# A gated recurrence and a channel-mix FFN on eight cores: the a stage and the first LN1 moved ahead, LN1's staging on VectorE alone, wo's evictions on ScalarE

## The chip, the cores and the metric

The kernel runs on the eight NeuronCores of one Trainium2 chip. Each core takes one of the eight sequences of the batch; nothing is exchanged between them. The metric is the device time in microseconds of the slowest core. The cores form two dies, 0 to 3 and 4 to 7.

## The reference, cut to what matters

```python
# x: (8, 2048, 1024) fp32; eight sequences, one per core
h = layernorm(x)
h = rsqrt(sum(h*h) + eps) * h * gamma * sqrt(1024)
q, k, v, g = h @ wq, h @ wk, h @ wv, h @ wg
a = sigmoid(h @ wa)
y[t] = a[t] * y[t-1] + k[t] * v[t]          # scan over the sequence
x = x + (q * y * silu(g)) @ wo

h = layernorm(x); hp = h shifted by one token
xr = mu_r * h + (1 - mu_r) * hp
xk = mu_k * h + (1 - mu_k) * hp
r = sigmoid(xr @ W_r.T)
x = x + r * (square(relu(xk @ W_k.T)) @ W_v.T)
```

## The kernel before, in words

A core works through its 2048 tokens in eight blocks b = 0 to 7 of 256 tokens. All nine weight matrices stay on the chip in bf16. A matrix product ("stage", `mm_stage`, line 190) is 64 matmuls of 128x128 by 128x256 into four of the eight PSUM banks (`pp`); the stages take banks 0 to 3 and 4 to 7 in turn, so a stage can start only when the stage before the last has been evicted. Stages are named by their weights: k, v, q, a, g, wo, and for the FFN r (`wrT`), fk (`wkT`), fv (`wvT`). The results of wo and fv are brought back to token order by 16 TensorE transposes (line 205) and added to x (`resid_stage`, line 220).

A layer norm has two parts. `ln_stats` makes the statistics on VectorE, with one square root on ScalarE (line 256). `ln_apply` writes the normalized tile in bf16: the first 128 tokens by VectorE (line 287), the other 128 by ScalarE (line 292). It goes to `stg1` for the first norm (LN1, in `phase_A`) and to `bfP` for the second (in `phase_E1`, called E1 below). Two DMA transposes on the queue of SP (line 302), the second of which waits for the first, bring it into feature order: `xhat_fm`, one half for even and one for odd blocks, or `xh2_fm`. The program calls `phase_A(b + 2)` twice in an iteration b, once behind yq and once at its end; both do all the work and write the same values. The a stage of block b + 2 reads the first result, its k, v, q and g stages the second.

Blocks overlap. Iteration b runs wo, transposes and E1 of block b; k, v, q of b + 1; the token shift of b (`phase_E2xr`, `phase_E2xk`); kv, scan and yq of b + 1; r and fk of b; g of b + 1; fv, transposes and residual of b; the a stage of b + 2; the store of b and the load of x for b + 3. Each engine goes through its instructions in program order. The order is written out by hand; there is no scheduler. A small planner (`Plan`) notes for every named region its last writer and its readers, and puts a wait in front of an instruction for each of them:

```python
        for w in writes:
            reg = self.regions.get(w)
            if reg:
                if reg["w"]:
                    deps.add(reg["w"])
                deps.update(reg["r"])
```

Each matmul is a token of its own, so a region that a stage has read has 64 readers. When the waits are made, a token is left out only if its engine has already waited for a higher count of the same semaphore; they are gone through in rising order and by the names of the semaphores (dq.., scalar, tensor, vector):

```python
            for (sem, val) in sorted(rec["deps"]):
                ...
                if k.get(sem, 0) < cnt:
                    k[sem] = cnt
                    w.append((sem, wv))
```

and `run_engine` issues one wait instruction (`wait_ge`, line 572) for each.

Of the kernel before, what the change touches and what calls it, by code (L numbers as in the profile page):

```python
# [10 lines left out]
D = 1024  # L11
T = 2048
L = 256
NB = T // L
# [83 lines left out]
def build_program():  # L98
    nc = bass.Bass("TRN2", target_bir_lowering=False,
                   dynamic_dma_scratch_size=4096)  # L100
# [30 lines left out]
    xh2_fm = sb("xh2_fm", [128, NCH * L], BF16)  # L131
    bfP = sb("bfP", [128, NCH * L], BF16)
    stg1 = sb("stg1", [128, NTI * D], BF16)
    y2b = sb("y2b", [128, NCH * L], BF16)
    fA = sb("fA", [128, NCH * L], F32)
    fB = sb("fB", [128, NCH * L], F32)
    fC = sb("fC", [128, NCH * L], F32)
    stats = sb("stats", [128, 36], F32)
    gam = sb("gam", [128, NCH], F32)
    mur = sb("mur", [128, NCH], F32)  # L140
    muk = sb("muk", [128, NCH], F32)
# [8 lines left out]
    p = Plan()  # L150
# [13 lines left out]
    def chunked(t):  # L164
        return t[:, :].rearrange("p (c l) -> p c l", c=NCH)
# [104 lines left out]
    def ln_apply(b, which, tag):  # L270
        par = b % 3
        ssc = SS1 if which == 1 else SS2
        xreg = "x%d" % par
        reg = "stats%d" % which
        dstreg = ("xhf%d" % (b % 2)) if which == 1 else "xh2"
        bbc = BB1 if which == 1 else BB2
        stg = stg1 if which == 1 else bfP
        streg = "stg1" if which == 1 else "bfP"
        for ti in range(NTI):
            b_ap = stats[:, bbc + ti:bbc + ti + 1]  # L280
            m_ap = stats[:, (MV1 if which == 1 else MV2) + 2 * ti:
                         (MV1 if which == 1 else MV2) + 2 * ti + 1]
            s_ap = stats[:, ssc + ti:ssc + ti + 1]
            xt = x_tm[:, par, ti * D:(ti + 1) * D]
            if ti == 0:
                p.op("vector", (lambda xt=xt, m_ap=m_ap, s_ap=s_ap, stg=stg:
                                nc.vector.tensor_scalar(stg[:, 0:D], xt, m_ap, s_ap,
                                                        OP.subtract, OP.mult)),
                     reads=[xreg + "t0", reg], writes=[streg], tag=tag)
            else:  # L290
                p.op("scalar", (lambda xt=xt, b_ap=b_ap, s_ap=s_ap, stg=stg:
                                nc.scalar.activation(stg[:, D:2 * D], xt,
                                                     AF.Identity, bias=b_ap, scale=s_ap)),
                     reads=[xreg + "t1", reg], writes=[streg], tag=tag)
        for ti in range(NTI):
            if which == 1:
                dst = xhat_fm[:, b % 2, :].rearrange(
                    "p (c l) -> p c l", c=NCH)[:, :, ti * 128:(ti + 1) * 128]
            else:
                dst = chunked(xh2_fm)[:, :, ti * 128:(ti + 1) * 128]  # L300
            p.op("sync", (lambda dst=dst, ti=ti, stg=stg:
                          nc.sync.dma_start_transpose(
                              dst, stg[:, ti * D:(ti + 1) * D])),
                 reads=[streg], writes=[dstreg], dma=True, tag=tag + "_dmaT")
# [43 lines left out]
    def phase_A(b):  # L348
        ln_stats(b, 1, "A%d" % b)
        ln_apply(b, 1, "A%d" % b)  # L350

    def phase_hoist_a(b):
        rr = ["xhf%d" % (b % 2)]
        rhs = lambda kc, b=b: xhat_view(b, kc)
        a_ids = mm_stage("wa", rhs, rr, "a%d" % b)
        for j in range(4):
            p.op("scalar", (lambda j=j, a_ids=a_ids: nc.scalar.activation(
                fhalf(fA, j), pp[a_ids[j]][:, :], AF.Sigmoid)),
                 reads=["pp%d" % a_ids[j]], writes=["fA%d" % j], tag="siga%d" % b)
# [48 lines left out]
    def phase_ygy2(b, g_ids):  # L408
        for j in range(4):
            p.op("vector", (lambda j=j, g_ids=g_ids: nc.vector.tensor_tensor(  # L410
                fhalf(fC, j), fhalf(fC, j), pp[g_ids[j]][:, :], OP.mult)),
                 reads=["pp%d" % g_ids[j], "fC"], writes=["fC"], tag="yg%d" % b)
        p.op("vector", (lambda: nc.vector.tensor_tensor(
            y2b[:, :], fC[:, :], bfP[:, :], OP.mult)),
             reads=["fC", "bfP"], writes=["y2b"], tag="y2_%d" % b)

    def phase_D(b):
        wo_ids = mm_stage("wo", (lambda kc: chunked(y2b)[:, kc, :]), ["y2b"],
                          "wo%d" % b)
        for j in range(4):  # L420
            p.op("vector", (lambda j=j, wo_ids=wo_ids: nc.vector.tensor_copy(
                fhalf(fB, j), pp[wo_ids[j]][:, :])),
                 reads=["pp%d" % wo_ids[j]], writes=["fB%d" % j], tag="woev%d" % b)
        t_ids = transpose_stage(fB, "fB", "Tattn%d" % b, sub=True)
        resid_stage(b, t_ids, "resid1_%d" % b)

    def phase_E1(b):
        ln_stats(b, 2, "E1_%d" % b)
        ln_apply(b, 2, "E1_%d" % b)

    def phase_E2xr(b):
        v = chunked(xh2_fm)
        pv = chunked(bfP)
        xr = chunked(y2b)
        p.op("vector", (lambda v=v, pv=pv: nc.vector.tensor_copy(
            pv[:, :, 1:L], v[:, :, 0:L - 1])),
             reads=["xh2"], writes=["bfP"], tag="prev%d" % b)
        if b == 0:
            p.op("vector", (lambda pv=pv: nc.vector.memset(pv[:, :, 0:1], 0.0)),
                 reads=[], writes=["bfP"], tag="prev0_%d" % b)  # L440
        else:
            p.op("vector", (lambda pv=pv: nc.vector.tensor_copy(
                pv[:, :, 0:1], carry2[:, :].rearrange("p (c o) -> p c o", o=1))),
                 reads=["carry2"], writes=["bfP"], tag="prev0_%d" % b)
        p.op("vector", (lambda v=v: nc.vector.tensor_copy(
            carry2[:, :].rearrange("p (c o) -> p c o", o=1), v[:, :, L - 1:L])),
             reads=["xh2"], writes=["carry2"], tag="carry2_%d" % b)
        tsh = chunked(stg1)
        p.op("vector", (lambda: nc.vector.tensor_sub(
            stg1[:, :], xh2_fm[:, :], bfP[:, :])),  # L450
             reads=["xh2", "bfP"], writes=["stg1"], tag="xr%d" % b)
        for c in range(NCH):
            p.op("vector", (lambda c=c, tsh=tsh, pv=pv, xr=xr:
                            nc.vector.scalar_tensor_tensor(  # L454
                                xr[:, c, :], tsh[:, c, :], mur[:, c:c + 1],
                                pv[:, c, :], OP.mult, OP.add)),
                 reads=["stg1", "mur", "bfP"], writes=["y2b"], tag="xr%d" % b)
    def phase_E2xk(b):
        v = chunked(xh2_fm)
        pv = chunked(bfP)  # L460
        tsh = chunked(stg1)
        for c in range(NCH):
            p.op("vector", (lambda c=c, tsh=tsh, pv=pv, v=v:
                            nc.vector.scalar_tensor_tensor(  # L464
                                v[:, c, :], tsh[:, c, :], muk[:, c:c + 1],
                                pv[:, c, :], OP.mult, OP.add)),
                 reads=["stg1", "muk", "bfP"], writes=["xh2"], tag="xk%d" % b)

    def phase_F1(b):
        xr_fn = lambda kc: chunked(y2b)[:, kc, :]  # L470
# [17 lines left out]
    def phase_F3(b):  # L488
        ks_fn = lambda kc: chunked(xh2_fm)[:, kc, :]
        v_ids = mm_stage("wvT", ks_fn, ["xh2"], "fv%d" % b)  # L490
        for j in range(4):
            p.op("vector", (lambda j=j, v_ids=v_ids: nc.vector.tensor_tensor(
                fhalf(fB, j), pp[v_ids[j]][:, :], fhalf(fB, j), OP.mult)),
                 reads=["pp%d" % v_ids[j], "fB%d" % j], writes=["fB%d" % j],
                 tag="fvev%d" % b)
# [28 lines left out]
    for b in range(NB):  # L524
        phase_D(b)
        phase_E1(b)
        if b + 1 < NB:
            vq[b + 1] = phase_hoist_kvq_mm(b + 1)
        phase_E2xr(b)
        if b + 1 < NB:  # L530
            phase_kvev(b + 1, vq[b + 1][0])
        phase_E2xk(b)
        if b + 1 < NB:
            phase_scan(b + 1)
            phase_yq(b + 1, vq[b + 1][1])
        if b + 2 < NB:
            phase_A(b + 2)
        phase_F1(b)
        phase_F2(b)
        if b + 1 < NB:  # L540
            g_ids_of[b + 1] = phase_hoist_g(b + 1)
            phase_ygy2(b + 1, g_ids_of[b + 1])
        phase_F3(b)
        phase_F4(b)
        if b + 2 < NB:
            phase_hoist_a(b + 2)
        phase_G(b)
        if b + 2 < NB:
            phase_A(b + 2)
# [88 lines left out]
```

How the kernel before makes its waits and increments, by code:

```python
        def run_engine(eng_name, eng):  # L569
            for rec in per_engine[eng_name]:
                for (sem, val) in rec["waits"]:
                    eng.wait_ge(sems[sem], val)
                ins = rec["emit"]()
                if rec["inc"]:
                    step = 16 if rec["sem"].startswith("dq") else 1
                    ins.then_inc(sems[rec["sem"]], step)
# [17 lines left out]
        @block.sync  # L594
        def _(eng):
            run_engine("sync", eng)
            for (sem, val) in final_waits:
                eng.wait_ge(sems[sem], val)
```

## Time and profile before

| | |
|---|---|
| median of three runs | 840.29 us (838.47 to 850.4) |
| profiled execution, its own time | 843.49 us |
| its span, core 2 (slowest) | 842.0 us |
| spans of the eight cores | 830.3 to 842.0 us |
| TensorE busy on core 2 | 590.1 us (70%) |
| VectorE busy | 410.1 us (49%) |
| ScalarE busy | 161.2 us (19%) |
| mean granted TensorE clock, core 2 | 0.903 |

The profiled execution is one run of the program; its time is that of the whole launch, the span goes from the first to the last instruction of the slowest core. Busy TensorE time counts pipelined matmuls, so a stage is best read by the distance from its first matmul to the next stage's. The first 134 us are the loading of the weights and the first norm; then come the eight iterations.

### The profile page before, as it was taken

To read this page: it belongs to the slowest core of one execution; us is meant where nothing else is said; L and a number is where in the kernel's file an instruction comes from. 1 tells how busy PE (TensorE), PEld (TensorE's weight loads), DVE (VectorE), ACT (ScalarE), POOL (GpSimd) and SP (SyncE) were. 2 spreads that over 40 slices of the span, in tenths; PEclk is the share of its full clock that TensorE was granted. 3 is DMA by queue.
4 is the path that set the end of the run, shared out by engine and by line. 5 is a ranking of instruction groups with operands and counts; after the bars stand their busy time and mean duration, and the time that the engine had idled before them with its cause. 6 is when DMAs were issued, how large, how long until landed. Compare 5 with 4: busy or idle time off the path is not lost.

```text
span 842.0 us, 13591 instructions; the slowest of 8 cores (830.3 to 842.0 us)
## 1 busy us (share of the span) xinstructions
PE 590.1 (70%) x4864; PEld 505.1 (60%) x4864; DVE 410.1 (49%) x726; ACT 161.2 (19%) x230; POOL 5.1 (1%) x13
## 2 busy tenths in 40 slices
PE   0000005899968899969796979796969797989065
PEld 0000004778757678868686868685858686879054
DVE  0001730334656358465756565556565656546342
ACT  0000011122032210521142123212321232131121
POOL 2000000000000000000000000000000000000000
PEclk9999999988877778999989999899999988999679
DMA  9999994001003210141014101320032002201101
GB/s 170 175 186 168 165 170 68 1 2 8 19 2 76 75 26 1 27 126 26 7 21 126 26 14 41 98 26 14 25 114 26 14 15 75 27 1 51 25 1 50
DMA packets 52881, 48.13 MB, mean 57 GB/s; under 512 B 47440, under 2 KB 47568, under 8 KB 51664
## 3 DMA queue, kind: packets, MB, share of 16 engines
q1 hardware_dynamic: 51520, 28.40, 14.3%
q0 software_dynamic: 1296, 18.87, 13.7%
q8 instruction: 40, 0.66, 0.3%
q14 instruction: 25, 0.20, 0.1%
HBM read 46.22 MB, written 8.39 MB: 65 GB/s over the span
## 4 chain that ended last, share of the span: by engine, by line
PE 54%; DVE 19%; DMA 11%; another core or an unknown queue 7%; issue 5%; ACT 3%; DVEq 1%; SPq 0%; ACTq 0%; POOLq 0%
PE pp L190 51%; DMA xhat_fm<-stg 7%; DVE fC L384 5%; PE pp L205 3%; DVE xh_fm L464 3%; DMA W_wk<-wk 3%; DMA xh_fm<-bfP 2%; DVE fB L375 1%; DVE y2b L454 1%; DVE stats L240 1%; DVE stats L237 1%; DVE fC L394 1%; ACT L473 1%; DVEq L572 1%
## 5 line engine op out<-in xcount | busy, mean ns | idle before, releaser
L190 PE MATMUL pp<-xhat_fm,W_wk 128*128 128x256 bf16 x512 | 73.9, 318 | 170.8 <-DMA xhat_fm<-stg 170.8
L190 PEld LDWEIGHTS pp<-xhat_fm,W_wk 128*128 128x128 bf16 x512 | 57.7, 114 | 186.3 <-issue 172.1
L190 PE MATMUL pp<-xhat_fm,W_wg 128*128 128x256 bf16 x512 | 69.7, 307 | 24.8 <-ACT fB L473 20.4
L190 PE MATMUL pp<-y2b,W_wrT 128*128 128x256 bf16 x512 | 62.2, 287 | 28.0 <-DVE y2b L454 27.6
L190 PEld LDWEIGHTS pp<-xhat_fm,W_wg 128*128 128x128 bf16 x512 | 55.6, 110 | 38.6 <-issue 26.6
L190 PEld LDWEIGHTS pp<-y2b,W_wrT 128*128 128x128 bf16 x512 | 52.4, 103 | 36.8 <-issue 28.5
L190 PE MATMUL pp<-xh_fm,W_wkT 128*128 128x256 bf16 x512 | 63.2, 289 | 15.5 <-DVE fC L394 15.5
L190 PEld LDWEIGHTS pp<-xh_fm,W_wkT 128*128 128x128 bf16 x512 | 52.7, 104 | 25.7 <-issue 17.0
L410 DVE TENSOR_TENSOR fC<-fC,pp 128x512 f32<-128x512 f32 x32 | 22.0, 688 | 87.0 <-PE pp L190 73.5
L190 PE MATMUL pp<-xhat_fm,W_wa 128*128 128x256 bf16 x512 | 61.4, 284 | 3.2 <-DMA xhat_fm<-stg 3.2
L190 PE MATMUL pp<-xh_fm,W_wvT 128*128 128x256 bf16 x512 | 58.6, 277 | 3.0 <-ACT xh_fm L484 3.0
L190 PE MATMUL pp<-xhat_fm,W_wq 128*128 128x256 bf16 x512 | 60.1, 281 | 0.0
L190 PE MATMUL pp<-xhat_fm,W_wv 128*128 128x256 bf16 x512 | 60.1, 281 | 0.0
L190 PE MATMUL pp<-y2b,W_wo 128*128 128x256 bf16 x512 | 60.1, 281 | 0.0
L190 PEld LDWEIGHTS pp<-xhat_fm,W_wa 128*128 128x128 bf16 x512 | 52.1, 102 | 11.1 <-issue 3.4
L190 PEld LDWEIGHTS pp<-xh_fm,W_wvT 128*128 128x128 bf16 x512 | 50.7, 99 | 9.7 <-issue 3.3
L190 PEld LDWEIGHTS pp<-xhat_fm,W_wq 128*128 128x128 bf16 x512 | 51.5, 101 | 7.2
L190 PEld LDWEIGHTS pp<-y2b,W_wo 128*128 128x128 bf16 x512 | 51.5, 101 | 7.2
L190 PEld LDWEIGHTS pp<-xhat_fm,W_wv 128*128 128x128 bf16 x512 | 51.5, 101 | 7.2
L256 ACT ACTIVATE stats<-stats 128x2 f32<-128x2 f32 x22 | 4.5, 203 | 238.7 <-DVE stats L249 178.1
L220 DVE TENSOR_TENSOR x_tm<-x_tm,pp 128x512 f32<-128x512 f32 x64 | 42.6, 686 | 8.3 <-PE pp L205 5.0
L384 DVE TENSOR_TENSOR_SCAN fC<-fA,carry,fB 128x256 f32<-128x256 f32 x56 | 42.0, 750 | 5.1
(56 smaller groups left out, 534.2 us busy)
## 6 DMA issues: line engine op xcount, KB each, us to landing
x_tm<-x SPq DMA_DIRECT2D x16, 512.0 KB, 5.3
out<-x_tm SPq DMA_DIRECT2D x8, 1024.0 KB, 4.4
W_wk<-wk POOLq DMA_DIRECT2D x1, 2048.0 KB, 22.0
W_wv<-wv POOLq DMA_DIRECT2D x1, 2048.0 KB, 35.7
W_wa<-wa POOLq DMA_DIRECT2D x1, 2048.0 KB, 49.7
W_wq<-wq POOLq DMA_DIRECT2D x1, 2048.0 KB, 63.7
W_wg<-wg POOLq DMA_DIRECT2D x1, 2048.0 KB, 75.9
W_wo<-wo POOLq DMA_DIRECT2D x1, 2048.0 KB, 88.9
```

The lines of the kernel that those rows point to most:

```text
L190: nc.tensor.matmul(pj[:, h * 256:(h + 1) * 256], wview(wname, kc, douc * 128, (douc + 1) * 128), rhs_fn(kc), start=st, stop=sp)),
L205: p.op("tensor", (lambda pj=pj, src=src, c=c: nc.tensor.transpose(pj[:, (c % 4) * 128:(c % 4 + 1) * 128], src, ident[:, :])), reads=rd, wr ...
L220: nc.vector.tensor_tensor(xv, xv, pp[t_ids[j]][:, :], OP.add)),
L237: p.op("vector", (lambda xt=xt: nc.vector.bn_stats(stats[:, 0:6], xt[:, 0:512])), reads=[xrg], writes=["statsB"], tag=tag)
L240: p.op("vector", (lambda xt=xt: nc.vector.bn_stats(stats[:, 6:12], xt[:, 512:1024])), reads=[xrg], writes=["statsB"], tag=tag)
L375: p.op("vector", (lambda j=j, v_ids=v_ids: nc.vector.tensor_tensor(fhalf(fB, j), pp[v_ids[j]][:, :], fhalf(fB, j), OP.mult)), reads=["pp%d ...
L384: p.op("vector", (lambda c=c, init=init: nc.vector.tensor_tensor_scan(f3(fC, c), f3(fA, c), f3(fB, c), init, OP.mult, OP.add)), reads=rd, ...
L394: p.op("vector", (lambda j=j, q_ids=q_ids: nc.vector.tensor_tensor(fhalf(fC, j), fhalf(fC, j), pp[q_ids[j]][:, :], OP.mult)), reads=["pp%d ...
L410: p.op("vector", (lambda j=j, g_ids=g_ids: nc.vector.tensor_tensor(fhalf(fC, j), fhalf(fC, j), pp[g_ids[j]][:, :], OP.mult)), reads=["pp%d ...
L454: nc.vector.scalar_tensor_tensor(xr[:, c, :], tsh[:, c, :], mur[:, c:c + 1], pv[:, c, :], OP.mult, OP.add)),
L464: nc.vector.scalar_tensor_tensor(v[:, c, :], tsh[:, c, :], muk[:, c:c + 1], pv[:, c, :], OP.mult, OP.add)),
L473: p.op("scalar", (lambda j=j, r_ids=r_ids: nc.scalar.activation(fhalf(fB, j), pp[r_ids[j]][:, :], AF.Sigmoid)), reads=["pp%d" % r_ids[j]], ...
```

## The change

Four things. LN1's staging tile `stg1` is written by VectorE alone, in both halves. The evictions of wo's four banks to `fB` go from VectorE to ScalarE. The difference h - hp of the token shift goes to `fC` (fp32) and no longer to `stg1` (bf16). And two calls move: the first `phase_A(b + 2)` from behind yq to behind E1, and the a stage of b + 2 with its sigmoids from behind the residual to the place ahead of fv. The second `phase_A(b + 2)` stays.

```diff
@@ ln_apply @@
-            if ti == 0:
-                p.op("vector", (lambda xt=xt, m_ap=m_ap, s_ap=s_ap, stg=stg:
-                                nc.vector.tensor_scalar(stg[:, 0:D], xt, m_ap, s_ap,
+            if ti == 0 or which == 1:
+                p.op("vector", (lambda xt=xt, m_ap=m_ap, s_ap=s_ap, stg=stg, ti=ti:
+                                nc.vector.tensor_scalar(stg[:, ti * D:(ti + 1) * D],
+                                                        xt, m_ap, s_ap,
                                                         OP.subtract, OP.mult)),
-                     reads=[xreg + "t0", reg], writes=[streg], tag=tag)
+                     reads=[xreg + "t%d" % ti, reg], writes=[streg], tag=tag)
@@ phase_D @@
-            p.op("vector", (lambda j=j, wo_ids=wo_ids: nc.vector.tensor_copy(
+            p.op("scalar", (lambda j=j, wo_ids=wo_ids: nc.scalar.copy(
                 fhalf(fB, j), pp[wo_ids[j]][:, :])),
@@ phase_E2xr, and the same reads in phase_E2xk @@
-        tsh = chunked(stg1)
+        tsh = chunked(fC)
         p.op("vector", (lambda: nc.vector.tensor_sub(
-            stg1[:, :], xh2_fm[:, :], bfP[:, :])),
-             reads=["xh2", "bfP"], writes=["stg1"], tag="xr%d" % b)
+            fC[:, :], xh2_fm[:, :], bfP[:, :])),
+             reads=["xh2", "bfP"], writes=["fC"], tag="xr%d" % b)
@@ the loop over b @@
         phase_D(b)
         phase_E1(b)
+        if b + 2 < NB:
+            phase_A(b + 2)
         if b + 1 < NB:
             vq[b + 1] = phase_hoist_kvq_mm(b + 1)
         phase_E2xr(b)
...
             phase_yq(b + 1, vq[b + 1][1])
-        if b + 2 < NB:
-            phase_A(b + 2)
         phase_F1(b)
         phase_F2(b)
         if b + 1 < NB:
             g_ids_of[b + 1] = phase_hoist_g(b + 1)
             phase_ygy2(b + 1, g_ids_of[b + 1])
+        if b + 2 < NB:
+            phase_hoist_a(b + 2)
         phase_F3(b)
         phase_F4(b)
-        if b + 2 < NB:
-            phase_hoist_a(b + 2)
         phase_G(b)
```

On TensorE, one iteration of before from r to k; then the same of the changed kernel.

```order
L190 MATMUL pp<-y2b,W_wrT 128x256 x64
L190 MATMUL pp<-xh_fm,W_wkT 128x256 x64
L190 MATMUL pp<-xhat_fm,W_wg 128x256 x64
L190 MATMUL pp<-xh_fm,W_wvT 128x256 x64
L205 MATMUL pp<-identity,fB 128x128 x16
L190 MATMUL pp<-xhat_fm,W_wa 128x256 x64
L190 MATMUL pp<-y2b,W_wo 128x256 x64
L205 MATMUL pp<-identity,fB 128x128 x16
L190 MATMUL pp<-xhat_fm,W_wk 128x256 x64
```

```order
L190 MATMUL pp<-y2b,W_wrT 128x256 x64
L190 MATMUL pp<-xh_fm,W_wkT 128x256 x64
L190 MATMUL pp<-xhat_fm,W_wg 128x256 x64
L190 MATMUL pp<-xhat_fm,W_wa 128x256 x64
L190 MATMUL pp<-xh_fm,W_wvT 128x256 x64
L205 MATMUL pp<-identity,fB 128x128 x16
L190 MATMUL pp<-y2b,W_wo 128x256 x64
L205 MATMUL pp<-identity,fB 128x128 x16
L190 MATMUL pp<-xhat_fm,W_wk 128x256 x64
```

The a stage stands between g and fv now, and nothing stands between the FFN's transposes and wo.

On ScalarE, from the a stage's sigmoids (line 357) over the second LN1 (square root in line 256, half tile in line 292) and E1 to the k evictions (line 366) and the first LN1; then the same of the changed kernel, where these lines have numbers one higher and wo's evictions are line 422.

```order
L357 ACTIVATE fA<-pp 128x512 x4
L256 ACTIVATE stats<-stats 128x2
L292 ACTIVATE stg<-x_tm,stats 128x1024
L256 ACTIVATE stats<-stats 128x2
L292 ACTIVATE bfP<-x_tm,stats 128x1024
L366 COPY fB<-pp 128x512 x4
L256 ACTIVATE stats<-stats 128x2
L292 ACTIVATE stg<-x_tm,stats 128x1024
L473 ACTIVATE fB<-pp 128x512 x4
```

```order
L358 ACTIVATE fA<-pp 128x512 x4
L256 ACTIVATE stats<-stats 128x2
L422 COPY fB<-pp 128x512 x4
L256 ACTIVATE stats<-stats 128x2
L293 ACTIVATE bfP<-x_tm,stats 128x1024
L256 ACTIVATE stats<-stats 128x2
L367 COPY fB<-pp 128x512 x4
L474 ACTIVATE fB<-pp 128x512 x4
```

The evictions of wo stand behind the square root of the second LN1; the first LN1's square root stands between E1 and the k evictions, and nothing is between those and the r stage's sigmoids (line 473 or 474).

On the queue of SP, one iteration of before from the load of x over the second LN1, E1 and the first LN1 to the store, with the semaphores that each row waits for; then the same of the changed kernel.

```order
L312 DMA x_tm<-x 128x1024 [waits sem_dq46]
L312 DMA x_tm<-x 128x1024
L302 DMA_TRANSPOSE xhat_fm<-stg1 128x8x128 [waits sem_dq45,sem_scalar,sem_tensor]
L302 DMA_TRANSPOSE xhat_fm<-stg1 128x8x128 [waits sem_dq49]
L302 DMA_TRANSPOSE xh2_fm<-bfP 128x8x128 [waits sem_scalar]
L302 DMA_TRANSPOSE xh2_fm<-bfP 128x8x128 [waits sem_dq51]
L302 DMA_TRANSPOSE xhat_fm<-stg1 128x8x128 [waits sem_dq41,sem_scalar]
L302 DMA_TRANSPOSE xhat_fm<-stg1 128x8x128 [waits sem_dq53]
L506 DMA out<-x_tm 128x2x1024 [waits sem_vector]
```

```order
L313 DMA x_tm<-x 128x1024 [waits sem_dq46]
L313 DMA x_tm<-x 128x1024
L303 DMA_TRANSPOSE xhat_fm<-stg1 128x8x128 [waits sem_dq45,sem_tensor,sem_vector]
L303 DMA_TRANSPOSE xhat_fm<-stg1 128x8x128 [waits sem_dq49]
L303 DMA_TRANSPOSE xh2_fm<-bfP 128x8x128 [waits sem_scalar,sem_tensor]
L303 DMA_TRANSPOSE xh2_fm<-bfP 128x8x128 [waits sem_dq51]
L303 DMA_TRANSPOSE xhat_fm<-stg1 128x8x128 [waits sem_dq41,sem_vector]
L303 DMA_TRANSPOSE xhat_fm<-stg1 128x8x128 [waits sem_dq53]
L507 DMA out<-x_tm 128x2x1024 [waits sem_vector]
```

The transposes stand in the same order. Those of the second LN1 wait for VectorE, behind TensorE, and no longer for ScalarE ahead of it; those of E1 wait for TensorE too, behind ScalarE.

## Rows read from the trace of the kernel before

**Rows 1.** The page's part 4, the chain that ended last, by line.

```profile
PE pp L190 51%; DMA xhat_fm<-stg 7%; DVE fC L384 5%; PE pp L205 3%; DVE xh_fm L464 3%; DMA W_wk<-wk 3%; DMA xh_fm<-bfP 2%; DVE fB L375 1%; DVE y2b L454 1%; DVE stats L240 1%; DVE stats L237 1%; DVE fC L394 1%; ACT L473 1%; DVEq L572 1%
```

**Rows 2.** Timeline of TensorE, core 2: start, us, instructions, [idle before <- releaser].

```profile
437.51 1.91 PE L205 MATMUL pp<-identity,fB 128*128 128x128 f32 x16
439.26 7.15 PE L190 MATMUL pp<-xhat_fm,W_wa 128*128 128x256 bf16 x64
446.25 7.15 PE L190 MATMUL pp<-y2b,W_wo 128*128 128x256 bf16 x64
...
461.71 9.68 PE L190 MATMUL pp<-xhat_fm,W_wk 128*128 128x256 bf16 x64 [6.57 <-DMA xhat_fm<-stg]
...
492.72 7.15 PE L190 MATMUL pp<-xh_fm,W_wkT 128*128 128x256 bf16 x64 [0.37 <-DVE fC L394]
504.17 8.81 PE L190 MATMUL pp<-xhat_fm,W_wg 128*128 128x256 bf16 x64 [4.30 <-ACT fB L473]
...
528.54 7.15 PE L190 MATMUL pp<-y2b,W_wo 128*128 128x256 bf16 x64
...
713.41 8.44 PE L190 MATMUL pp<-xhat_fm,W_wk 128*128 128x256 bf16 x64 [6.25 <-DMA xhat_fm<-stg]
...
746.30 8.81 PE L190 MATMUL pp<-xh_fm,W_wkT 128*128 128x256 bf16 x64 [3.50 <-DVE fC L394]
```

**Rows 3.** Timeline, core 2: the second LN1 on VectorE, ScalarE and SP.

```profile
445.29 0.17 DVE L249 TENSOR_SCALAR stats<-stats 128x2 f32<-128x2 f32 x1
...
446.28 0.82 SPq L312 DMA_DIRECT2D x_tm<-x  x2
...
448.42 0.20 ACT L256 ACTIVATE stats<-stats 128x2 f32<-128x2 f32 x1
...
449.33 0.81 DVE L287 TENSOR_SCALAR stg<-x_tm,stats 128x1024 bf16<-128x1024 f32 x1
...
450.24 1.24 ACT L292 ACTIVATE stg<-x_tm,stats 128x1024 bf16<-128x1024 f32 x1 [1.62 <-DVE stg L287]
...
455.13 4.40 SPq L302 DMA_TRANSPOSE xhat_fm<-stg  x2
```

**Rows 4.** Timeline, core 2: E1 of b = 3, then E1 of b = 7.

```profile
463.10 1.24 ACT L292 ACTIVATE bfP<-x_tm,stats 128x1024 bf16<-128x1024 f32 x1 [1.62 <-DVE bfP L287]
464.41 4.34 SPq L302 DMA_TRANSPOSE xh_fm<-bfP  x2
...
470.73 0.69 DVE L435 COPY bfP<-xh_fm 128x2040 bf16<-128x2040 bf16 x1 [7.72 <-DMA xh_fm<-bfP]
...
788.81 1.24 ACT L292 ACTIVATE bfP<-x_tm,stats 128x1024 bf16<-128x1024 f32 x1 [1.62 <-DVE bfP L287]
793.30 4.33 SPq L302 DMA_TRANSPOSE xh_fm<-bfP  x2
```

**Rows 5.** Timeline of VectorE, core 2: y2's product, the token shift's difference, its first products.

```profile
432.42 2.29 DVE L413 TENSOR_TENSOR y2b<-fC,bfP 128x2048 bf16<-128x2048 f32 x1
...
471.99 1.23 DVE L449 TENSOR_TENSOR stg<-xh_fm,bfP 128x2048 bf16<-128x2048 bf16 x1
473.33 4.61 DVE L454 SCALAR_TENSOR_TENSOR y2b<-stg,mur,bfP 128x256 bf16<-128x256 bf16 x8
```

**Rows 6.** Timeline of ScalarE, core 2: the table load ahead of the last E1's square root.

```profile
785.69 1.28 ACT L256 ACT_TABLE_LOAD   x1 [22.89 <-DVE stats L253]
```

**Rows 7.** Timeline of VectorE, core 2: first residual piece and first statistics of E1, b = 3.

```profile
454.27 0.69 DVE L220 TENSOR_TENSOR x_tm<-x_tm,pp 128x512 f32<-128x512 f32 x1
...
457.20 0.69 DVE L237 BATCH_NORM_STATS2 stats<-x_tm 128x6 f32<-128x512 f32 x1
```

**Rows 8.** Windows, core 2, then core 0: us, busy PE, PEld, DVE, ACT, POOL, PEclk, DMA, GB/s.

```profile
190.00:210.00 20.00, 20.00 (x155) 16.92 (x153) 9.15 (x17) 4.66 (x7) 0.00 (x0) 0.81 0.10 8
180.00:200.00 20.00, 20.00 (x185) 18.09 (x184) 10.18 (x16) 2.51 (x5) 0.00 (x0) 1.00 0.00 1
```

**Rows 9.** Timeline of TensorE, core 2: the a and wo stages at the end of b = 0.

```profile
270.82 9.88 PE L190 MATMUL pp<-xhat_fm,W_wa 128*128 128x256 bf16 x64 [3.15 <-DMA xhat_fm<-stg]
280.52 8.58 PE L190 MATMUL pp<-y2b,W_wo 128*128 128x256 bf16 x64
```

More of the change, by code:

```diff
@@ L456, in phase_E2xr @@
                                 pv[:, c, :], OP.mult, OP.add)),
-                 reads=["stg1", "mur", "bfP"], writes=["y2b"], tag="xr%d" % b)
+                 reads=["fC", "mur", "bfP"], writes=["y2b"], tag="xr%d" % b)
     def phase_E2xk(b):
@@ L460, in phase_E2xk @@
         pv = chunked(bfP)
-        tsh = chunked(stg1)
+        tsh = chunked(fC)
         for c in range(NCH):
@@ L466, in phase_E2xk @@
                                 pv[:, c, :], OP.mult, OP.add)),
-                 reads=["stg1", "muk", "bfP"], writes=["xh2"], tag="xk%d" % b)
+                 reads=["fC", "muk", "bfP"], writes=["xh2"], tag="xk%d" % b)
     def phase_F1(b):
```

## The prediction

> **What bounds the kernel now.** First the granted clock and the chain of waits. By the chain [rows 1], the stage loop of TensorE (line 190) holds 51% of the span, the transposes of LN1 7%, the scan 5%, the product of line 464 3%: no engine alone sets the time, the path changes over from one to another. So I read one loop iteration on TensorE, b = 3 of core 2 [rows 2]. A stage of 64 matmuls takes 6.99 us at full clock (a at 439.26 to wo at 446.25), 16 transposes take 1.75 (437.51 to 439.26). The iteration has nine stages and two transpose groups, 9 x 6.99 + 2 x 1.75 = 66.4 us, but from wo at 446.25 to the next wo at 528.54 there are 82.3 us. The rest are two large waits and the clock behind them: 6.57 us before the k stage, which then takes 9.68 instead of 7.15, and 4.30 us before the g stage, which then takes 8.81. From k at 461.71 to k at 713.41 are three iterations of 83.9 us.
>
> Between the fk stage and what precedes it there is a second limit: VectorE. From the start of wo to the start of fk it is 46.47 us, and fk waited for the yq product on VectorE. That stretch is a chain through VectorE and DMA: wo, eviction, transposes, residual at +8.02, LN statistics at +10.95 [rows 7], bf16 tile written at +18.09, DMA transposes at +18.16, prev copy at +24.48 [rows 4], then token shift, kv, xk, scan and yq.
>
> **The waits of the SP queue.** Before the transposes of the second LN1 the gap is odd: ScalarE ends its half of stg1 at 450.24 + 1.24 = 451.48, yet the transposes start at 455.13 [rows 3]. The 3.65 us between them belong to no engine. The order shows a wait on TensorE's semaphore in that row, and the planner's code says what it is: a write waits for each earlier reader of the region, one wait instruction for each of the 64 matmuls of the a stage. They were satisfied long before; SP steps through them one by one, behind the wait for ScalarE, since the names are sorted. Without them, in the E1 of the iteration, the tile ends at 464.34 and the DMA starts at 464.41, 0.07 us later. The E1 of b = 7 has 64 such waits (for fv) already: tile at 790.05, DMA at 793.30, 3.25 us [rows 4]. So 64 satisfied waits cost 3.2 to 3.6 us when they stand behind the last event.
>
> **The change part by part, from wo's start.**
> 1. The a stage moves ahead of fv. It then stands between g and fv, where its input (the first LN1) is there, and wo follows the transposes. Nothing of TensorE's own work is saved. But it covered, ahead of wo, the second LN1 of the same block. Now the second LN1's statistics end 6.20 us after wo starts (445.29 + 0.17 against the stage at 439.26 that follows the transposes now) [rows 2, 3]. ScalarE must load the square root's table, and a table load does not run ahead of the wait of its instruction: the one at 785.69 comes after 22.89 us of idling for VectorE and takes 1.28 [rows 6]. So 6.3 + 1.3 = 7.6 for the square root, and the second half of stg1, now on VectorE, starts where ScalarE's did, 1.82 later, and takes 0.81: 10.2.
> 2. SP has store, load x (at +7.02, 0.82 long) and then its 64 waits for the a stage, this time ahead of the last event: 7.84 + 3.4 = 11.2 for the transposes. From their start to the k stage it is 6.58 us (455.13 to 461.71): k starts at +17.8, where PE was free at +8.75. The wait is 9.1 us, longer than the 6.57 of before.
> 3. The four evictions of wo go to ScalarE, behind that square root: they start at 7.8 and, at no more than the 0.69 of a VectorE piece of the same size [rows 7], end by 10.5, the first two by 9.2; VectorE is held by the second LN1 until 10.2 anyway. The residual starts at 10.3 instead of 8.02: **+2.3 us** on VectorE's chain.
> 4. The E1 transposes get 64 new waits, for the fv stage. The a stage used to be the last reader that SP had waited for, and it came after fv; now it comes before, and no longer covers fv. They stand behind the wait for E1's tile: **+3.25 us**, from b = 1 to 6; b = 7 has them already, b = 0 has none.
> 5. The first LN1 of b + 2 moves from behind yq to behind E1. On VectorE it takes 5.0 us of statistics (as E1's, 457.20 to 462.19, which is 0.91 ahead of ScalarE's 463.10 [rows 4, 7]) and two halves of 0.91, 6.8 in all, in the shade of E1's transposes, which last 6.3 us plus the 3.25 of item 4 (in b = 0, 6.3 plus the 1.3 of ScalarE's half). Cost nothing; without that shade 6.8. Its transposes queue behind E1's; more below. In its old place it held back ScalarE's sigr and so g by 4.30 us. That wait goes, and with it the cold clock, 8.81 - 7.15 = 1.66.
> 6. The token shift's difference goes to fC in fp32. The bf16 subtraction of 2048 elements takes 1.23 us, the fp32/bf16 product of the same size 2.29 [rows 5]: **+1.06 us**. The 16 products that read it I cost at nothing: they take 4.61 us for 8 x 256 elements, 2.3 ns each, more than that fp32 product (1.1 ns), so they do not run at a rate that two-byte inputs gave them. At the excess of the subtraction they would cost 16 x 256 / 2048 x 1.06 = 2.1 us more per iteration; that is the upper end.
>
> Sum: wo to fk = 46.47 + 2.3 + 3.25 + 1.06 = 53.1 us. TensorE is ready for fk earlier: 17.8 + 9.7 (k at the low clock) + 3 x 6.99 = 48.5. So fk waits 4.6 us, and by the g stage after 4.30 us, and fk itself in b = 6 (8.81 after 3.50) [rows 2], it pays 1.7 for the clock (the k stage after 6.57 us: 2.5); I take 1.9. From fk to the next wo four stages, the transposes and this: 4 x 6.99 + 1.75 + 1.9 = 31.6. The period is 84.7 against 82.3, +2.4; against the mean of 83.9, whose excess over 82.3 partly comes back and partly lies in the waits that go, less, at least +0.8. I take +2.1, near the iteration that I can follow row by row.
>
> In b = 0 the gain is whole: the a stage waits 3.15 us there for the transposes of its first LN1 and then takes 9.88 instead of the 8.58 of the wo stage behind it [rows 9]. That LN1 is now made right behind E1, ahead of xr, kv, xk, scan and yq; its transposes stand behind the waits for five stages on SP, 320 of them (16 to 18 us by the price above), but the r, fk and g stages alone give 3 x 6.99 = 21 us, and the waits now run ahead of the wait for VectorE. 3.15 + 1.3 - 1.06 = 3.4 us less. b = 1 to 5: 5 x 2.1 = 10.5 more. b = 6 (fk 8.81 already, no LN1 to come): 2.3 + 3.25 + 1.06 + 0.2 = 6.8 more. b = 7: 1.06 more. Together -3.4 + 10.5 + 6.8 + 1.1 = +15.0 us. The profiled execution took 843.49 (span 842.0) and would take 858.5; it lies 3.2 above the median of 840.29, so the forecast is **855 us**, 1.8% more. Two per cent is about what a measurement of this kernel can tell from no change.
>
> **A rule against this.** In rows of core 2 the clock stands at 0.81 over 190 to 210 us and its stages take some 8.58 us [rows 9], while core 0 is at 1.00 from 180 to 200 with TensorE busy all 20 us [rows 8]. 0.81 lies between the two levels of 1.2 and 2.4 GHz; both cores did dense matmuls, so density alone does not bring it. The Trainium skill (TensorE: Matmul & The Clock Gate, "Seeing it yourself") has a peak-current limiter that takes a whole die to 13/16 of the clock when a third core of it runs dense matmuls. Core 0's row speaks against that for core 0 and 2, which share a die.
>
> **The rivals.**
> - *The new waits cost nothing* (SP fetches and clears satisfied waits fast here, or item 4's order differs). Then wo to fk is 49.8, TensorE is ready at 48.5, the clock holds: period 49.8 + 29.7 = 79.5, some 5.2 less for six iterations: 855 - 31 = 824. Against it stands the 3.25 of b = 7. Chance 0.12.
> - *The square root's table is loaded early.* Then 1.3 us less for six iterations: 847. Against it stands [rows 6]. 0.08.
> - *Slower: the transposes of the first LN1 run into E1's.* They are issued as soon as SP has issued E1's second one, which still has 1.9 us to go (the pair takes 6.32 us, 464.41 to 470.73, so 3.1 each, and its issue 4.34, so 1.2 for the second [rows 4]). If both share the DMA engines it lands up to 1.9 later, and all of that is on VectorE's chain: 6 x 1.9 = 11, 866. It decides (2%, 857) from 0.4 us per iteration on. For it: two kinds of transfers never overlapped there before. Against: one queue serves them in order. 0.17.
> - *Slower: the low clock of 0.81.* The four stages and transposes behind fk would take 8.58 instead of 7.15: 4 x 1.43 + 0.4 = 6.1 per iteration; in two iterations, as in this trace, +12 (867), in all seven 43 (898). The stages ahead of fk have 4.6 us of slack. 0.11.
> - The forecast as summed: 0.52, its own range 846 to 864 (each period 1.5 us shorter or longer, by the price of the clock, 1.7 to 2.8, and of the products of item 6).
>
> **How the numbers follow.** The range is 824 to 868: the first rival's centre on one side, the third and a short spell of the fourth on the other; what is left out is half of the first and most of the fourth. Faster by over 2% (under 823.5): half of the first rival and a little for a cost that I overlooked on the path of before, 0.10. Slower by over 2% (over 857.1): both slower rivals, 0.28, and the upper part of the forecast, 0.15: 0.43, some of it given back to the uncertain price of the clock: 0.40. Within: 0.50.
>
> **What would show it.** In the changed profile g must start without a wait and a follow it; fk must wait 4 to 5 us for yq, k about 9 us for the transposes of the second LN1. E1's transposes must start over 3 us after ScalarE's half. The subtraction must take about 2.3 us, and wo's evictions must start behind a table load. I am wrong if wo to fk comes out at 50 or less, or if E1's prev copy comes over 6.5 us after its transposes' start.

## The result and the profile after

The changed kernel takes 851.45 us (median of ten runs, 849.37 to 879.24), the kernel before 839.02 in the same ten rounds; the ratio is 1.0145, with a 95% interval of 1.0126 to 1.0164. It is 1.5% slower, clearly more than nothing and less than 2%. Runs in which a die was disturbed, such as the one of 879.24, are not in the ratio.

The chain that ended last, by line, in the page of the changed kernel (span 850.1 us, core 6):

```profile
PE pp L190 50%; DMA xhat_fm<-stg 7%; DVE fC L385 6%; PE pp L205 3%; DVE xh_fm L465 3%; DMA xh_fm<-bfP 3%; DMA W_wk<-wk 3%; DVE y2b L455 2%; DVE fB L376 2%; DVE fC L450 1%; DVEq L573 1%; DVE fC L395 1%; DVE x_tm L220 1%; DVE stats L240 0%
```

It has hardly moved against [rows 1]; the new entries are the E1 transposes (3% instead of 2%) and the token shift's difference, line 450. TensorE's timeline says more. These are the end of b = 0, and then b = 3, of core 6:

```profile
251.32 7.15 PE L190 MATMUL pp<-xhat_fm,W_wa 128*128 128x256 bf16 x64
...
267.04 7.15 PE L190 MATMUL pp<-y2b,W_wo 128*128 128x256 bf16 x64
...
440.68 7.15 PE L190 MATMUL pp<-y2b,W_wo 128*128 128x256 bf16 x64
449.58 2.06 PE L205 MATMUL pp<-identity,fB 128*128 128x128 f32 x16 [1.74 <-DVE stats L265]
458.21 8.68 PE L190 MATMUL pp<-xhat_fm,W_wk 128*128 128x256 bf16 x64 [6.57 <-DMA xhat_fm<-stg]
...
495.36 8.87 PE L190 MATMUL pp<-xh_fm,W_wkT 128*128 128x256 bf16 x64 [7.07 <-DVE fC L395]
504.06 7.15 PE L190 MATMUL pp<-xhat_fm,W_wg 128*128 128x256 bf16 x64
511.05 7.15 PE L190 MATMUL pp<-xhat_fm,W_wa 128*128 128x256 bf16 x64
518.03 7.15 PE L190 MATMUL pp<-xh_fm,W_wvT 128*128 128x256 bf16 x64
...
526.77 7.15 PE L190 MATMUL pp<-y2b,W_wo 128*128 128x256 bf16 x64
```

Read them against [rows 2]. The four stages from fk to the next wo now run in a row: g has lost its wait of 4.30 us and its 8.81. In b = 0 the a stage has no wait ([rows 9] had 3.15). In exchange fk waits 7.07 us for the yq product, where it waited 0.37, and takes 8.87; over all cores and b = 1 to 5 it waits 5.9 us in the mean, where it waited 1.2. In the windows over fk (the columns are PE, PEld, DVE, ACT, POOL busy with their counts, then the granted clock):

```profile
495.40:497.00 1.60, 1.60 (x8) 1.09 (x9) 1.39 (x3) 0.00 (x0) 0.00 (x0) 0.50 0.00 0
499.00:504.00 5.00, 5.00 (x48) 4.48 (x47) 0.00 (x0) 1.79 (x3) 0.00 (x0) 1.00 0.01 3
```

Behind 7.07 us without a matmul it starts at 0.50, the level of 1.2 GHz, and is back at 1.00, 2.4 GHz, from 499.00 at the latest. From wo to fk it is 54.68 us instead of 46.47, from fk to wo 31.41 instead of 35.82. Over all eight cores and b = 1 to 5 the means are 53.98 instead of 47.15 and 31.84 instead of 35.85 (from the starts of these stages): a period of 85.8 instead of 83.0 us.

Where the 54.68 go is in the timeline of the other engines of core 6, the second LN1 first, then E1 and the token shift:

```profile
446.72 0.17 DVE L249 TENSOR_SCALAR stats<-stats 128x2 f32<-128x2 f32 x1
447.19 0.82 SPq L313 DMA_DIRECT2D x_tm<-x  x2
447.24 1.28 ACT L256 ACT_TABLE_LOAD   x1 [14.44 <-DVE stats L249]
448.54 0.20 ACT L256 ACTIVATE stats<-stats 128x2 f32<-128x2 f32 x1
448.65 2.03 ACT L422 COPY fB<-pp 128x512 f32<-128x512 f32 x4
...
449.46 1.74 DVE L287 TENSOR_SCALAR stg<-x_tm,stats 128x1024 bf16<-128x1024 f32 x2
...
451.11 2.86 DVE L220 TENSOR_TENSOR x_tm<-x_tm,pp 128x512 f32<-128x512 f32 x4
451.72 4.41 SPq L303 DMA_TRANSPOSE xhat_fm<-stg  x2
453.88 0.69 DVE L237 BATCH_NORM_STATS2 stats<-x_tm 128x6 f32<-128x512 f32 x1
...
459.78 1.24 ACT L293 ACTIVATE bfP<-x_tm,stats 128x1024 bf16<-128x1024 f32 x1 [1.62 <-DVE bfP L287]
...
464.28 5.82 SPq L303 DMA_TRANSPOSE xh_fm<-bfP  x2
...
472.21 0.69 DVE L436 COPY bfP<-xh_fm 128x2040 bf16<-128x2040 bf16 x1 [5.68 <-DMA xh_fm<-bfP]
...
473.38 2.29 DVE L450 TENSOR_TENSOR fC<-xh_fm,bfP 128x2048 f32<-128x2048 bf16 x1
...
475.78 4.62 DVE L455 SCALAR_TENSOR_TENSOR y2b<-fC,mur,bfP 128x256 bf16<-128x256 f32 x8
```

The table load starts behind the statistics and not ahead of them; wo's evictions stand behind it and the square root; the two halves of stg1 hold VectorE until 451.2, and the residual starts there, 10.43 us behind wo (451.11 - 440.68), where it was at 8.02 [rows 7]. E1's tile is ready at 459.78 + 1.24 = 461.02, its transposes start at 464.28: 3.26 us in which VectorE works on the first LN1 of b + 2 and TensorE on k, but nothing runs that these transposes need, where [rows 4] had 0.07. The difference takes 2.29 us instead of 1.23 [rows 5]; the products that read it take 4.62 for eight, as before.

### The profile page after: what moved, and what is told of

Same layout as the page of the kernel before. It is cut to its first block, busy times and chain, and to the rows that moved or that the text cites. A ratio compares the mean times of both kernels' runs of the same rounds, so it can differ in the third digit from the quotient of the medians.

```text
span 850.1 us, 14129 instructions; the slowest of 8 cores (843.4 to 850.1 us)
## 1 busy us (share of the span) xinstructions
PE 574.6 (68%) x4864; PEld 496.9 (58%) x4864; DVE 409.7 (48%) x708; ACT 162.0 (19%) x248; POOL 5.1 (1%) x13
## 4 chain that ended last, share of the span: by engine, by line
PE 53%; DVE 19%; DMA 12%; another core or an unknown queue 7%; issue 5%; ACT 1%; DVEq 1%; SPq 0%; ACTq 0%; POOLq 0%
PE pp L190 50%; DMA xhat_fm<-stg 7%; DVE fC L385 6%; PE pp L205 3%; DVE xh_fm L465 3%; DMA xh_fm<-bfP 3%; DMA W_wk<-wk 3%; DVE y2b L455 2%; DVE fB L376 2%; DVE fC L450 1%; DVEq L573 1%; DVE fC L395 1%; DVE x_tm L220 1%; DVE stats L240 0%
## 5 line engine op out<-in xcount | busy, mean ns | idle before, releaser
L190 PE MATMUL pp<-xh_fm,W_wkT 128*128 128x256 bf16 x512 | 73.0, 315 | 42.7 <-DVE fC L395 42.7
L190 PEld LDWEIGHTS pp<-xh_fm,W_wkT 128*128 128x128 bf16 x512 | 57.1, 112 | 58.4 <-issue 44.5
L190 PE MATMUL pp<-xhat_fm,W_wg 128*128 128x256 bf16 x512 | 58.9, 277 | 4.4 <-DVE fC L395 4.4
L190 PE MATMUL pp<-xhat_fm,W_wq 128*128 128x256 bf16 x512 | 57.2, 273 | 0.4 <-ACT fB L367 0.4
L190 PEld LDWEIGHTS pp<-xhat_fm,W_wg 128*128 128x128 bf16 x512 | 50.9, 100 | 11.2 <-issue 4.6
L190 PE MATMUL pp<-xhat_fm,W_wa 128*128 128x256 bf16 x512 | 57.2, 273 | 0.0
L190 PE MATMUL pp<-xhat_fm,W_wv 128*128 128x256 bf16 x512 | 57.2, 273 | 0.0
L190 PE MATMUL pp<-y2b,W_wo 128*128 128x256 bf16 x512 | 57.2, 273 | 0.0
L493 DVE TENSOR_TENSOR fB<-pp,fB 128x512 f32<-128x512 f32 x32 | 22.0, 691 | 69.1 <-PE pp L190 61.6
L190 PEld LDWEIGHTS pp<-xhat_fm,W_wa 128*128 128x128 bf16 x512 | 50.1, 98 | 5.8
```

The lines of the kernel that those rows point to most:

```text
L190: nc.tensor.matmul(pj[:, h * 256:(h + 1) * 256], wview(wname, kc, douc * 128, (douc + 1) * 128), rhs_fn(kc), start=st, stop=sp)),
```

## The experiments

The theory from here on: TensorE is not the bound; the time is VectorE's chain from wo to fk plus four stages, and the a stage's move lengthens that chain at two places that the diff doesn't show, the waits for fv in front of E1's transposes and the second LN1 in front of the residual. The main rival: the 3.26 us are no waits but something of the DMA transposes themselves, and the second LN1 acts through k. Each kernel was timed in three rounds beside the kernel before (839.42 us for the first four, 837.84 for the others, 839.02 beside the changed kernel), so differences between kernels of different groups are good to some 1.6 us.

**One wait for each semaphore, in the changed kernel.**

```diff
             w = []
-            for (sem, val) in sorted(rec["deps"]):
+            top = {}
+            for (sem, val) in rec["deps"]:
+                top[sem] = max(top.get(sem, 0), val)
+            for (sem, val) in sorted(top.items()):
```

> The changed kernel with one wait for each semaphore (the highest count) in place of 64 or 320 waits in a row; the order of all work and the events waited for are the same. My theory (the 64 satisfied waits for fv stand on VectorE's chain): E1's transposes start 0.1 us behind ScalarE's half instead of 3.3, in b = 1 to 7, so 7 x 3.25 = 23 us less, and since fk's wait falls from 6.3 to about 3 us, part of the low clock behind it goes too, up to 2 us in each of six iterations: 817 to 829 us. Rival A (the satisfied waits are free, the 3.3 us are something else, such as the time that a DMA transpose needs to start behind another): no change, 851, and the 3.3 us stay. Rival B (TensorE then becomes the bound at 48.5 us from wo to fk): not below 815.

822.72 us, ratio 0.9793 (0.9776 to 0.9811): 28.7 us less than the changed kernel, and faster than before. Timeline of core 4, E1 of b = 3 and then fk and wo of b = 4 and 5:

```profile
448.95 1.24 ACT L296 ACTIVATE bfP<-x_tm,stats 128x1024 bf16<-128x1024 f32 x1 [1.63 <-DVE bfP L290]
450.33 4.87 SPq L306 DMA_TRANSPOSE xh_fm<-bfP  x2
...
515.13 7.15 PE L193 MATMUL pp<-y2b,W_wo 128*128 128x256 bf16 x64
565.10 7.15 PE L193 MATMUL pp<-xh_fm,W_wkT 128*128 128x256 bf16 x64 [3.02 <-DVE fC L398]
...
594.78 7.15 PE L193 MATMUL pp<-y2b,W_wo 128*128 128x256 bf16 x64
```

Tile at 450.19, transposes at 450.33: 0.14 us. With the waits merged the gap is gone, so the waits were the gap. From wo to fk it is 49.97 here and 50.49 in the mean (53.98 with the waits), and where fk waits only some 3 us it can keep the full clock, 7.15, so fk to wo falls too, from 31.84 to 30.74 in the mean. Seven times 3.3, and five or six times 1.1, are the 28.7. Rival A is out. Two limits: fk kept the full clock in 15 of the 48 stages of b = 1 to 6 and took mostly 8.81 in the others, and the edit merges the waits of all engines, not of SP alone; the residual starts 0.3 us earlier too (10.14 behind wo).

**The same in the kernel before.**

> The kernel before with one wait for each semaphore. My theory: the second LN1's transposes start 3.3 to 3.6 us earlier in each iteration, but fk is bound by VectorE's chain, which has no such waits except in b = 7, so this only moves the idle time from k to fk; what counts are b = 7 (3.25) and b = 0, where 320 waits stood before the first LN1's transposes (a waited 5.6 us on the cores at full clock, and took 1.7 more): together 10 us, about 829 us. The wait before k falls from 6.5 to 3 us and k's clock improves, with no gain from it. Rival (the waits in front of the second LN1 are on the path, as the chain of waits says): 6 x 3.4 = 20 us more, 809. If the satisfied waits are free: 839.

820.28 us, ratio 0.9764 (0.9739 to 0.9788). Neither figure: 19 us less, where I had 10 and the rival 30. TensorE of core 1, b = 3:

```profile
431.68 7.15 PE L193 MATMUL pp<-y2b,W_wo 128*128 128x256 bf16 x64
...
443.56 8.50 PE L193 MATMUL pp<-xhat_fm,W_wk 128*128 128x256 bf16 x64 [2.98 <-DMA xhat_fm<-stg]
...
479.78 9.14 PE L193 MATMUL pp<-xh_fm,W_wkT 128*128 128x256 bf16 x64 [6.76 <-DVE fC L397]
491.23 7.15 PE L193 MATMUL pp<-xhat_fm,W_wg 128*128 128x256 bf16 x64 [2.31 <-ACT fB L476]
...
513.94 7.15 PE L193 MATMUL pp<-y2b,W_wo 128*128 128x256 bf16 x64
```

The wait before k fell from 6.57 to 2.98, and wo to fk did not move (47.27 in the mean, 47.15 before): the idle time went to fk, 6.76, as expected. What I missed lies behind fk. The lower clock now falls on fk, 9.14, where g waits for ScalarE in any case, and g waits less (2.31) and runs at 7.15 instead of 8.81; fk to wo is 34.36 instead of 35.85 in the mean, 7.5 us in five iterations. With 8.3 us from the first k stage to the second wo (b = 0) and 3.6 in b = 7, both means over the cores, that is the 19. So without the satisfied waits the kernel before takes 820 and the changed one 823: the change gains nothing there either.

**The a stage back behind the residual, the rest as changed.**

```diff
             phase_ygy2(b + 1, g_ids_of[b + 1])
-        if b + 2 < NB:
-            phase_hoist_a(b + 2)
         phase_F3(b)
         phase_F4(b)
+        if b + 2 < NB:
+            phase_hoist_a(b + 2)
         phase_G(b)
```

> The changed kernel with the a stage back behind the FFN's transposes; everything else as changed (first LN1 behind E1, staging on VectorE, wo's evictions on ScalarE, fp32 difference). My theory: the a stage's move is what costs. With it back, the second LN1 and its table load are done under the a stage, and fv is covered by the waits for a, so E1's transposes have none: wo to fk 46.5 + 1.1 = 47.6 to 48.4 instead of 54.4, and fk to wo stays at about 32 since g no longer waits: a period of about 80 to 80.5 us instead of 86.5, and 5.5 us less in b = 6: 812 to 816 us. Rival (the first LN1's new place and the fp32 difference cost as much as the a stage's): about 835 to 840. Rival (the a stage's move pays, as it fills TensorE): over 851.

814.94 us, ratio 0.9704 (0.9689 to 0.9719). TensorE of core 7, b = 3:

```profile
430.65 7.15 PE L190 MATMUL pp<-y2b,W_wo 128*128 128x256 bf16 x64
...
478.82 8.78 PE L190 MATMUL pp<-xh_fm,W_wkT 128*128 128x256 bf16 x64 [7.07 <-DVE fC L395]
487.44 7.15 PE L190 MATMUL pp<-xhat_fm,W_wg 128*128 128x256 bf16 x64
...
510.15 7.15 PE L190 MATMUL pp<-y2b,W_wo 128*128 128x256 bf16 x64
```

Wo to fk is 48.17 (48.39 in the mean), fk to wo 31.33, though fk waits as long as in the changed kernel. The a stage's move alone costs 36.5 us beside the others, and these together bring 24.5. They pay behind fk: fk to wo is 31.77 us in the mean, where it was 35.85 before, since g never waits (3.61 us in the mean before), while wo to fk is 1.2 longer. Which of them frees g was not run apart; the first LN1's new place is what the prediction names, and LN1's half tile has left ScalarE too. The move that looks best in TensorE's order is the one that loses.

**The difference in bf16 again**, in the changed kernel, in half of fC's bytes.

```diff
-        tsh = chunked(fC)
+        tsb = fC[:, 0:NCH * L // 2].bitcast(BF16)
+        tsh = tsb.rearrange("p (c l) -> p c l", c=NCH)
```

> The changed kernel with the token shift's difference in bf16 again, in the first half of fC's bytes; reads by the 16 products are bf16 again as well. My theory: the subtraction takes 1.23 us again instead of 2.29, the products stay at 0.58 each, 8 x 1.06 = 8.5 us less: 843. Rival (the products too are slowed by fp32): up to 2.1 us more per iteration, 826 to 830. Rival (the difference is hidden by other work): 851.

843.56 us, ratio 1.0052 (1.0032 to 1.0071): 7.9 less. VectorE of core 7:

```profile
469.72 1.22 DVE L451 TENSOR_TENSOR fC<-xh_fm,bfP 128x2048 bf16<-128x2048 bf16 x1
471.05 4.61 DVE L456 SCALAR_TENSOR_TENSOR y2b<-fC,mur,bfP 128x256 bf16<-128x256 bf16 x8
```

The subtraction alone is paid for; the products take the same 4.61 either way. The price in the time, 7.9, lies between seven and eight times the 1.07 that it is shorter (7.5 and 8.6), so this instruction lies on the path in nearly every iteration.

**Wo's evictions on VectorE again**, in the changed kernel (`p.op("vector"` and `tensor_copy` in `phase_D`).

> The changed kernel with wo's evictions on VectorE again. My theory: VectorE is held by the second LN1 until 10.2 us behind wo's start, so the four evictions would stand behind it there and in front of the residual, 4 x 0.7 = 2.9 us more on VectorE's chain in b = 1 to 6, 17 us: 868. Rival (ScalarE's evictions are what delays the residual, since they stand behind the table load and the square root): 838 to 845.

869.37 us, ratio 1.0377 (1.0355 to 1.0399): 17.9 more, or 19.4 by the two ratios. VectorE of core 4 in b = 3, whose wo starts at 449.48:

```profile
449.48 7.15 PE L190 MATMUL pp<-y2b,W_wo 128*128 128x256 bf16 x64
...
457.98 1.74 DVE L287 TENSOR_SCALAR stg<-x_tm,stats 128x1024 bf16<-128x1024 f32 x2
459.63 2.48 DVE L422 COPY fB<-pp 128x512 f32<-128x512 f32 x4
...
462.29 0.69 DVE L220 TENSOR_TENSOR x_tm<-x_tm,pp 128x512 f32<-128x512 f32 x1 [0.19 <-PE pp L205]
```

The evictions queue behind the second LN1 and put the residual at 12.8 us. So their move to ScalarE was needed once the a stage had gone, and it hides part of what that costs.

**The changed kernel without the second LN1** (the last `phase_A(b + 2)` of the loop left out; the first one has written the same values).

> The changed kernel without the second LN1 of each iteration (its values are those of the first). Nothing of it stands between the FFN's residual and wo's evictions then, and k needs no wait. My theory: the residual starts at 8.0 us behind wo instead of 10.4, but E1's square root must now load the table itself, 1.3 us, so VectorE's chain is 1.1 us shorter in six iterations, while the waits on SP for fv stay: 844 us, and TensorE idles 14 to 16 us before fk. If the second LN1 were the bound through k (its wait of 6.6 to 7 us with the clock behind it is 8.5 us): 800.

Ratio 1.0122 (1.0099 to 1.0145), by which it takes 848 us, where I had 844 and the rival 800. That is 2 to 3 less than the changed kernel, whose interval (1.0126 to 1.0164) overlaps this one, though some 6.8 us of VectorE's work per iteration are gone. Core 0, b = 3:

```profile
439.02 7.15 PE L190 MATMUL pp<-y2b,W_wo 128*128 128x256 bf16 x64
...
447.04 0.69 DVE L220 TENSOR_TENSOR x_tm<-x_tm,pp 128x512 f32<-128x512 f32 x1 [5.71 <-PE pp L205]
...
454.04 1.28 ACT L256 ACT_TABLE_LOAD   x1 [7.13 <-DVE stats L253]
```

The residual is at 8.02 again, and E1's square root pays for the table: 53 us from wo to fk, 1 less than with both LN1. K has no wait at all here on any core (b = 1 to 5), and next to nothing comes of it; in the kernel before, too, wo to fk did not move when the wait before k, TensorE's largest in an iteration, was cut to 2.98.

**The parts that paid, together**: the a stage back, one wait for each semaphore, the difference in bf16; first with both LN1, then with one.

> The changed kernel with the a stage back, one wait for each semaphore and the difference in bf16; both LN1 kept. My theory: 815 of the version with the a stage back alone, less 3.3 us for the waits of b = 7 and less 8.5 us for the subtraction: 803. If the 6 to 7 us of idling before fk bring a cold clock whatever is done, no change of that.

805.52 us (803 expected), ratio 0.9619 (0.9601 to 0.9637), the fastest of all. Core 0, b = 3:

```profile
427.22 7.15 PE L193 MATMUL pp<-y2b,W_wo 128*128 128x256 bf16 x64
...
474.79 9.24 PE L193 MATMUL pp<-xh_fm,W_wkT 128*128 128x256 bf16 x64 [6.64 <-DVE fC L398]
483.87 7.15 PE L193 MATMUL pp<-xhat_fm,W_wg 128*128 128x256 bf16 x64
...
506.57 7.15 PE L193 MATMUL pp<-y2b,W_wo 128*128 128x256 bf16 x64
```

> The changed kernel with the a stage back, one wait for each semaphore, the difference in bf16, and without the second LN1. Beside the next one it tells what the second LN1 is worth here: with it gone, VectorE and SP have less to do, but the table load of 1.3 us comes onto the chain of E1. My theory: 1.3 us longer in six iterations than with both: 811. Rival (less work is faster): under 803.

809.31 us, ratio 0.9658 (0.9643 to 0.9673): 3.8 slower than with the superfluous LN1. ScalarE of core 3:

```profile
443.62 1.28 ACT L259 ACT_TABLE_LOAD   x1 [7.13 <-DVE stats L256]
```

That load stands in E1 now, behind the statistics; with the second LN1 it was done ahead of E1, right behind the a stage's sigmoids and under wo (428.09 on core 0 of the version above, wo at 427.22). 1.3 us in six iterations would be 7.8; the measured 3.8 is half of it. E1's transposes take 6.26 us here in the mean (prev copy against their start) and 6.84 with both LN1, which is about the other half. Why they do is open: the second LN1 alone does not explain it, for in the changed kernel without it they take 7.04.

## Why the prediction was right

The time forecast was 855, the measured one 851.45; each against its own baseline, +14.7 forecast (from 840.29) and +12.4 measured (from 839.02). The direction and the terms of the period stood; the term of b = 0 did not, and that the total came so near is in part luck (last item).

- *Item 4, the new waits, +3.25.* 3.26 us in the row above; 3.45 in the mean over the cores and b = 1 to 6, some being 3.65 as [rows 3]. Shown by merging them: 0.14. The first rival is out.
- *Items 1 and 3, +2.3.* The residual is at 10.43 (10.3 forecast). The table load waits for the statistics; the second rival is out.
- *Item 2.* k starts at 17.53 us behind wo (17.8), and it does not matter. The text named 9.1 us of wait; the rows have 8.3, 1.74 before the last transposes and 6.57 before k. That it does not matter is shown by the run in which k has no wait.
- *Item 5.* The first LN1 of b + 2 is hidden in the shade of E1's transposes: the step on the path is nil, and g's wait is gone. By the text's own sign, a prev copy over 6.5 us behind its transposes' start, it would be wrong here: it is 6.85 us in the mean of the cores and 7.93 in the rows of core 6 above. But the sign was taken from one row of 6.32; the kernel before has 6.87 in the mean, with a scatter from 6.3 to 8.0. The changed kernel's transposes are no slower than that, and the third rival's extra time did not come.
- *Item 6, +1.06.* 2.29 us, 7.9 us in the experiment, and nothing for the products.
- *The sum.* Wo to fk 53.98 in the mean, forecast 53.1 on a base of 46.47. The mean of before is 47.15, and with that base the sum gives 53.8. Fk waits 5.6 to 7.1 us on core 6 in b = 1 to 5 (5.9 in the mean of the cores) and not 4.6: the chain there came out at 52.9 to 55.5, k started 0.3 earlier in b = 3, and its stage took 8.7 to 10.0 where the sum had 9.7.
- *The clock behind fk* was taken at 1.9 us. Fk takes 9.35 in the mean, 2.2 more than at full clock; fk to wo is 31.84, forecast 31.6.
- *The low clock of 0.81.* No stage of the changed kernel's trace that starts without a wait takes more than 7.15 us, on any core, and the mean clocks are 0.917 to 0.921. The fourth rival did not come; what brings that clock is not shown here.
- *b = 0* gave more than the 3.4 forecast: core 2, from which it was read, ran b = 0 at the clock of 0.81. From the first k stage to the second wo, core 0 of before takes 139.6 us (133.87 to 273.48), core 6 of after 131.1: 8.5. That is a mis-sized term, by 5 us; the period's +2.8 over the five full iterations instead of +2.1 took 3.5 of them back. Two misses of opposite sign, so the total is nearer than its parts.

## What to carry to other kernels

Count the wait instructions in front of an instruction, not the events: a planner that puts one wait for each reader of a region, 64 for one stage, can turn a moved read into 3.3 us behind the last event, which no row of any engine shows. Merge them first: both kernels gain more by that (19 and 29 us) than the change moves. And find what a stage covers before moving it into a gap: here the a stage held wo back until a norm's statistics were done, and without it the norm and its table load came between wo and the residual. Ahead of fk another engine's chain set the date: a gap closed there on TensorE reopened in front of fk, and only what lengthened or shortened that chain (waits, 1.06 us of a subtraction, the evictions) moved the time. Behind fk it was otherwise: the wait that g lost there did pay.

## What I had not expected of the hardware

Leaving out a whole superfluous norm per iteration made the best version 3.8 us slower, since it had also loaded the square root's table ahead of time. And a longer idle stretch costs no more clock when it falls in front of a stage whose successor waits anyway: in the kernel before with merged waits fk took 9.14 us instead of 7.15, and fk to wo still fell from 35.85 to 34.36. And satisfied waits on SP are not free: with 64 of them merged into one, E1's transposes start 0.13 us behind the tile instead of 3.26 or 3.65, some 50 to 56 ns for each wait left out. Why the same 64 waits come in two sizes is open.
